# A fused RWKV-style block: the first token mix folded into its weights, Wo's product beside the statistics, spare products, and new orders of all engines

## What is computed

```python
x = x + attn_a(layernorm(x))     # mixer A
x = x + ffn(layernorm(x))        # 8 experts
x = x + attn_b(layernorm(x))     # mixer B
x = x + ffn(layernorm(x))        # the same 8 experts

# attn_a: xx is x one token back
xk, xv, xr = (x * m + xx * (1 - m) for m in (mix_k, mix_v, mix_r))
kv, r = (xk @ Wk.T) * (xv @ Wv.T), xr @ Wr.T
state = kv + exp(time_decay) * state          # a scan over tokens
out = layernorm(r * (time_first * kv + state)) * ln_g + ln_b
return out @ Wo.T

# ffn: every expert on every token, weighted by two softmaxes over experts
h = silu(x @ w_gate[e]) * (x @ w_up[e]);  out = sum_e (h @ w_down[e]) * cw[e]
```

## Time and profile before

| | |
|---|---|
| runs | 925.91, 926.3, 928.23 us; median 926.3 |
| profiled execution | 925.21 us, of it span 923.2 us, mean granted clock 0.972 |
| TensorE busy | 850.2 us (92%), 5170 instructions |
| VectorE | 562.0 us (61%), 927 |
| ScalarE | 401.0 us (43%), 874 |
| GpSimd | 409.2 us (44%), 287 |

### The profile page before, as it was taken

The page is one execution under the profiler, slowest core; times in us unless marked ns, Lnnn a source line. Parts: engine busy times, 40 slices in busy tenths (PEclk is TensorE's granted clock), DMA queues, the critical chain, the costliest instruction groups (busy, mean ns, idle before and its releaser), DMA issues.

```text
span 923.2 us, 13835 instructions
## 1 busy us (share of the span) xinstructions
PE 850.2 (92%) x5170; PEld 717.0 (78%) x5170; DVE 562.0 (61%) x927; ACT 401.0 (43%) x874; POOL 409.2 (44%) x287
## 2 busy tenths in 40 slices
PE   3399999989898999999999799799999799999998
...
DMA packets 20710, 35.87 MB, mean 39 GB/s; under 512 B 3062, under 2 KB 9636, under 8 KB 20644
## 3 DMA queue, kind: packets, MB, share of 16 engines
...
...
## 4 chain that ended last, share of the span: by engine, by line
PE 54%; DVE 9%; issue 2%; ACT 1%; POOL 0%; DVEq 0%; ACTq 0%; POOLq 0%
PE bank L1222 53%; DVE states L1882 1%; DVE sh_buf L1662 1%; DVE w_a L1884 1%; DVE backs L1865 1%; DVE scr L1890 1%; DVE state L1786 0%; PE bank L1236 0%; DVE work L1761 0%; DVE state L1794 0%; ACT sh_buf L1049 0%; ACT w_sb L1137 0%; ACT backs L1121 0%; POOL work L888 0%; DVE stats L1548 0%
## 5 line engine op out<-in xcount | busy, mean ns | idle before, releaser
L1662 DVE TENSOR_TENSOR sh_buf<-sh_buf,bank 128x512 f32<-128x512 f32 x256 | 172.8, 684 | 264.2 <-PE bank L1222 225.6
L1222 PEld LDWEIGHTS bank<-w_down,sh_buf 128*128 128x128 f32 x2048 | 274.9, 193 | 47.9 <-DVE sh_buf L1662 24.7
L1222 PE MATMUL bank<-w_down,sh_buf 128*128 128x128 f32 x2048 | 294.8, 281 | 16.2 <-DVE sh_buf L1662 16.2
L1049 ACT ACTIVATE sh_buf<-bank 128x512 f32<-128x512 f32 x256 | 152.3, 598 | 304.7 <-PE bank L1222 227.9
L1222 PE MATMUL bank<-z_lo,w_hi 128*128 128x512 f32 x512 | 234.5, 458 | 0.9 <-DVE z_lo L1673 0.9
L1222 PE MATMUL bank<-z_hi,w_lo 128*128 128x512 f32 x512 | 204.0, 398 | 0.0
L1222 PE MATMUL bank<-z_hi,w_hi 128*128 128x512 f32 x512 | 203.3, 397 | 0.0
L946 POOL TENSOR_TENSOR x<-x,y_weighted 128x512 f32<-128x512 f32 x63 | 88.5, 1405 | 224.7 <-ACT y_weighted L1163 224.7
L1222 PEld LDWEIGHTS bank<-z_hi,w_hi 128*128 128x128 f32 x512 | 96.9, 189 | 23.4
L1222 PEld LDWEIGHTS bank<-z_lo,w_hi 128*128 128x128 f32 x512 | 98.6, 193 | 14.5 <-issue 3.9
L1222 PEld LDWEIGHTS bank<-z_hi,w_lo 128*128 128x128 f32 x512 | 98.6, 193 | 9.0 <-issue 1.2
...
## 6 DMA issues: line engine op xcount, KB each, us to landing
...
```

Source lines behind the costliest of these rows:

```text
L1049: act.activation(s_buf[:, m % 2, :], bank_of("gate", m)[:], ACT.Silu).then_inc(S["silu_done"], 1)
L1222: return pe.matmul(dst, lhs, rhs, start=start, stop=stop, **kw)
L1662: dve.tensor_tensor(h_buf[:, m % 4, :], s_buf[:, m % 2, :], bank_of("up", m)[:], ALU.mult).then_inc(S["h_done"], 1)
```

## The change

- **Token mix.** For the first batch of unit 0 (s = 0) there is no `mix`. ScalarE scales the three weight matrices of mixer A by the mix and by one minus it (`fold`, six matrices w_mix), and each of k, v and r is two products, one with the tokens and one with the tokens one back. VectorE makes one minus the mix, a centring matrix and a copy of the identity (`fold`). Batches 1 to 3 are as before; GpSimd's first split now waits for the mix of batch 1.
- **Wo.** TensorE makes a centred Wo scaled by ln_g, and ln_b times Wo, once (`output_weights`); ScalarE copies them. `mid_out` multiplies the mixer's result with it directly, with no wait for the norm; `mid_stats` only takes statistics, and `mid_add` applies the factor of each token from PSUM in four scalar_tensor_tensor. The bias is added to x before (`mid_bias`). Centring, scaling, the back transposes and the affine copy are gone for all four blocks.
- **Spare products** on TensorE, whose results nobody reads: 8 before the making of Wo, 8 before the first k, 40 short ones before the first `mid_T`, 28 before the first experts' transposes, 5 before the first gate.
- **Order inside a product.** `split_product` takes z_lo last; the first gate of a pass waits for z_hi, and for z_lo ahead of its last part.
- **Last link.** The 64th link of unit 1 is left out (`last_link`); its result was read by no unit.
- **Orders.** LEAD has new numbers (one list for 64 expert and other groups), as have WEIGHT, CHUNK_TIME and NEAR; PE_SUMS has other steps; the plan's rule for a low clock starts at 45 us (WARM). STICK is 0 and has no effect.

```diff
 LN_EPS_B = 1e-6
...
 WIDE, WIDE_POOL, FULL_POOL, SUM, SUM_STEP = 1.22, 1.95, 2.34, 1.22, 2.05
 PE_SUM = 1.75
-PE_SUMS = dict(T2=[0, 0, 1, 1, 1, 1, 0, 1, 1, 1, 1, 0, 1, 1, 1, 1], W2=[1, 1, 1, 1, 1, 0, 1, 1, 1, 1, 1, 1, 1, 1, 1, 1])
...
 TABLE_LOAD, HOP, START = 1.28, 0.07, 5.0
-CHUNK_TIME = 2.40
-WEIGHT = dict(pe=1.60, act=1.10, dve=1.31, pool=1.10, sp=1.02)
-LEAD = dict(experts=[15.0, -87.7, -93.1, -11.1, -35.5, 8.6, -5.6, 25.5, -52.3, -13.0, -39.8, -122.8, -61.2, -22.7, -10.9, 22.3, -14.4, -56.4, -44.1, -49.8, 37.7, -42.7, 21.0, 9.8, 40.8, 84.3, 89.0, -55.9, -103.9, -34.9, -59.6, 18.9, 76.3, 38.8, -73.9, -81.8, 5.4, 3.3, 25.3, -0.7, -80.3, 79.8, -96.5, -10.0, 41.0, -27.3, 31.4, 42.4, -52.9, 114.6, -88.2, 168.1, -118.3, -81.8, -173.8, 100.3, 113.4, -0.3, -65.5, -148.7, -96.1, 101.2, -151.0, 92.9], front=[-69.8, -115.2, -57.1, 115.0], steps=[62.2, 84.4, -31.2, -8.9], back=[18.5, 79.3, 4.9, 12.1], chain=[-16.1, 67.7], other=[57.8])
...
@@ -133,6 +135,8 @@
...
+        if c == 0:
+            after += (on("dve", "ffn_low", q),)
...
                      *((on("pe", "gate", i // 2 * FC - 9),) if i >= 6 else (on("pe", "r", 1),) if i >= 2 else ()), port=True)]
     return out
...
+            ready += (on("pe", "r", s - 2), on("dve", "inner", s - 2)) if s >= 2 else ()
+            out += [dve(("mix", s), 2.95, *ready, port=True),
+                    pe(("kv", s), 1.87, on("dve", "mix", s), *order, takes=((("k", s), on("act", "kv", s)), (("v", s), on("dve", "scan", s))))]
...
 def middle(q):
+
     u = q // BU
     inner = (on("dve", "inner", 2 * u), on("dve", "inner", 2 * u + 1))
-    out = norm("mid", q, (on("pe", "mid_T", q),), 0.78, (on("pe", "mid_out", q - 1),) if q else (), norm=0.7, centre=False)
-    if q:
...
+            pool(("mid_stats", q), 1.35, on("dve", "mid_stats", q)),
+            pe(("mid_out", q), 0.82, *inner, on("pe", "mid_T", q), on("act", "wo"), *((on("pe", "mid_out", q - 1),) if q else ()), takes=((("mid_out", q), on("dve", "mid_add", q)),)),
+            dve(("mid_bias", q), 0.69, on("act", "wo"), on("dve", "in_centre", q)),
+            dve(("mid_add", q), 0.95, on("pool", "mid_stats", q), on("pe", "mid_out", q), on("dve", "mid_bias", q), *last)]
 
 
 def ffn_input(q):
@@ -228,7 +237,7 @@
     u = j // BU
     z_after = ()
     if j == 0:
-        z_after = (on("dve", "biases"), on("pe", "mid_out", 3), on("pool", "split", 2 * E - 1))
+        z_after = (on("dve", "biases"), on("pe", "mid_out", 3), on("dve", "mid_bias", 3), on("pool", "split", 2 * E - 1))
     elif j == BU:
         z_after = (on("dve", "block_end", j - 1), on("pool", "T4", G * j - 1))
...
 
+def last_link(u):
+
+    return NCH - 1 - (u == UNITS - 1)
...
-            if begin > START + GATE and sum(min(b, begin) - max(a, begin - GATE) for a, b in self.busy) < GATE / 2:
+            if begin > WARM and sum(min(b, begin) - max(a, begin - GATE) for a, b in self.busy) < GATE / 2:
...
-        k_sb, nT = readout[:, 0:BT], readout[:, BT:2 * BT]
+        k_sb = readout[:, 0:BT]
+        spare = z_lo[:, 1, 0:P]
+        wo_centred, wo_bias, centring, wo_scaled = (readout[:, BT + i * C:BT + (i + 1) * C] for i in range(4))
...
+        w_mix = work[:, 0:6 * C].rearrange("p (i c) -> p i c", i=6)
...
+            def mid_scale(q):
+
+                pool.wait_ge(S["mid_mv"], q + 1)
+                step.inc(pool.tensor_scalar(mid_rstd[:, 0, :], mid_mv[:, :, 1], LN_EPS, None, ALU.add))
+                step.wait()
+                pool.tensor_tensor(mid_rstd[:, 1, :], mid_rstd[:, 0, :], neg_half[:].broadcast_to((P, G)), ALU.pow).then_inc(S["mid_rstd"], 1)
...
+            def fold():
+
+                act.wait_ge(S["unmix_rdy"], 1)
+                for i, nm in enumerate(("mix_k", "mix_v", "mix_r")):
+                    step.inc(act.activation(w_mix[:, i, :], w_a[:, i, :], ACT.Copy, scale=col(nm)))
+                    ins = act.activation(w_mix[:, 3 + i, :], w_a[:, i, :], ACT.Copy, scale=unmix[:, i:i + 1])
+                    if i < 2:
+                        step.inc(ins)
+                ins.then_inc(S["folded"], 1)
...
+            def scale_wo():
+                act.activation(wo_scaled, w_a[:, 3, :], ACT.Copy, scale=col("ln_g")).then_inc(S["wo_scaled"], 1)
+
+            def copy_wo():
+                act.wait_ge(S["wo_made"], 1)
+                act.activation(readout[:, BT:BT + 2 * C], bank_of("wo")[:, 0:2 * C], ACT.Copy).then_inc(S["wo_rdy"], 1)
...
+
+                for _ in range(n):
+                    mm(bank[:, 0:P], ident[:], ident[:])
...
+            def keep_busy_short(bank, n):
+
+                for _ in range(n):
+                    mm(bank[:, 0:P], spare, spare)
...
+                take(name)
+                if j == 0 and kind in SPARE:
+                    keep_busy(bank_named[name], SPARE[kind])
                 pe.wait_ge(S["ln_norm"], n + 1)
-                take(name)
...
+            def mixed_product(bank, s, i):
+
+                if s:
+                    return mm(bank, w_a[:, i, :], mixed[s % 2][i])
+                mm(bank, w_mix[:, i, :], xn[:, 0, 1:1 + TU], stop=False)
+                return mm(bank, w_mix[:, 3 + i, :], xn[:, 0, 0:TU], start=False)
...
+                if s == 0:
+                    take(BANK["k", s])
+                    keep_busy(bank_named[BANK["k", s]], 8)
+                    pe.wait_ge(S["folded"], 1)
+                    pe.wait_ge(S["ln_out"], max(LN["in", k] for k in range(BU)) + 1)
+                else:
+                    pe.wait_ge(S["mixed_rdy"], s)
...
-                    ins = mm(bank_named[name][:], w_a[:, i, :], mixed[s % 2][i])
+                    ins = mixed_product(bank_named[name][:], s, i)
...
+                take(name)
+                if q == 0:
+                    keep_busy_short(bank_named[name], 40)
                 pe.wait_ge(S["kvr_used"], B * (u + 1))
-                take(name)
...
+            def output_weights():
+
+                name = BANK["wo",]
+                take(name)
+                keep_busy(bank_named[name], 8)
+                pe.wait_ge(S["unmix_rdy"], 1)
+                pe.wait_ge(S["wo_scaled"], 1)
+                mm(bank_named[name][:, 0:C], centring, wo_scaled)
+                mm(bank_named[name][:, C:2 * C], col("ln_b").broadcast_to((P, P)), w_a[:, 3, :]).then_inc(S["wo_made"], 1)
+                free[name] = (S["wo_rdy"], 1)
...
-                pe.wait_ge(S["ln_out"], LN["mid", q] + 1)
+                pe.wait_ge(S["wo_rdy"], 1)
+                pe.wait_ge(S["kvr_used"], B * (u + 1))
                 take(name)
                 for i in range(G):
-                    ins = mm(bank_named[name][:, i * P:(i + 1) * P], nT[:, i * P:(i + 1) * P], w_a[:, 3, :])
+                    ins = mm(bank_named[name][:, i * P:(i + 1) * P],
+                             oT.rearrange("c (u p i) -> c u i p", u=UNITS, i=LU)[:, u, G * g + i, :], wo_centred)
...
+            def split_product(bank, lo, hi, q, first=False):
+
+                mm(bank, lo, z_hi[:, q % 2, :], stop=False)
+                mm(bank, hi, z_hi[:, q % 2, :], start=False, stop=False)
+                if first:
+                    pe.wait_ge(S["z_low"], q + 1)
+                return mm(bank, hi, z_lo[:, q % 2, :], start=False)
...
+                name = BANK["gate", g]
+                take(name)
+                if g == 0:
+                    keep_busy(bank_named[name], 5)
                 if c == 0:
-                    pe.wait_ge(S["z_low"], q + 1)
+                    pe.wait_ge(S["ln_out"], LN["ffn", q] + 1)
                 if q == 0 and f == 0:
                     pe.wait_ge(S["w_split"], 2 * e + 2)
-                name = BANK["gate", g]
-                take(name)
-                split_product(bank_named[name][:], w_lo[:, e, 0, cols_f], w_hi[:, e, 0, cols_f], q).then_inc(S["g_full"], 1)
+                split_product(bank_named[name][:], w_lo[:, e, 0, cols_f], w_hi[:, e, 0, cols_f], q, c == 0).then_inc(S["g_full"], 1)
...
+            def fold():
+                dve.wait_ge(S["w_in_a"], 16 * 5)
+                dve.wait_ge(S["const"], 2)
+                step.inc(dve.tensor_scalar(centring, ident[:], -1.0 / C, None, ALU.add))
+                step.inc(dve.tensor_copy(spare, ident[:]))
+                step.wait()
+                dve.tensor_scalar(unmix[:], cols[:, COLS.index("mix_k"):COLS.index("mix_k") + 3], -1.0, 1.0, ALU.mult, ALU.add).then_inc(S["unmix_rdy"], 1)
...
-                if b == 0:
+                if b == 0 or s == 1:
                     dve.wait_ge(S["ln_out"], max(LN["in", BU * u + k] for k in range(BU)) + 1)
-                if s == 0:
-                    dve.wait_ge(S["w_in_a"], 16 * 5)
...
+            def mid_statistics(q):
+                dve.wait_ge(S["ot_full"], q + 1)
+                for i in range(G):
+                    ins = dve.bn_stats(mid_stats[:, i, :], inner(q)[:, i, :])
+                    if i < G - 1:
+                        step.inc(ins)
+                step.wait()
```

(28 more changed lines are left out.)

111 lines of the change are left out of this document (62 added, 49 removed).

## The result

| | before | after |
|---|---|---|
| runs, us | 925.91, 926.3, 927.11, 928.23; median 926.7 | 917.1, 917.45, 918.91, 919.09; median **918.18** |
| ratio | | 0.9913, 95% interval 0.9898 to 0.9928 |
| profiled execution | 925.21, span 923.2 | 917.1, span 915.4 |
| first hidden product starts | 49.16 | 42.38 |
| from there to the end of the span | 874.0 | 873.0 |

What follows compares the result with a forecast made beforehand. It took TensorE to bound the body, with holes of a few us, but not the opening. 925.2 - 8.5 (opening) - 2.1 (body) - 1 (orders) = 913.6 profiled; with 1.1 to the median, 914.5 us, range 905 to 921.5.

Steps and rivals of the forecast that it cites:

- Up to the normalised input: Start of the opening: the fold on VectorE costs an estimated 0.45 us; normalised input ready at 14.3 instead of 13.82.
- First token mix: Opening, first k and v products: mix moved into the weights, k's copy at 19.0 against 20.59, 1.65 us earlier.
- GpSimd beside VectorE: First mixer: GpSimd's splits may slow VectorE's steps, 0 to 0.76 us, taken as 0.35; mixer ends at 27.85.
- Middle: From the first mixer's end to z_hi: pieces sum to 8.55 us plus 0.3; z_hi at 36.7, 7.3 earlier.
- sign that I had named: Before the first experts' transposes: forecast is wrong if TensorE runs spare products when the scaled tile is ready.
- z_hi to the first hidden product: VectorE and ScalarE chain with a table load, 43.97 to 49.16, claimed unmoved by the clock; first hidden product 7.3 us earlier.
- Five more wide parts: By the first hidden product TensorE can have five more parts behind it, at 0.24 us each: 1.2 us.
- Body: After the opening: less TensorE work and the last link gain 2.1 us; new orders of all engines taken as -1.
- its two Wo products stay: Unit 1's middle: loses 8 transposes, 0.9 us of TensorE, while the two Wo products remain.
- a body that does not follow: Rival: opening gains as forecast but the body gives back some 5 us: 919 to 923; chance 0.13.
- Rival 2: Body: the new orders take out a quarter of the idle, 904 to 906 us; chance 0.12.
- Rival 3: Opening: clock stays at its lower level and spare products become the bound; first gate 18 us later, 941; chance 0.04.

## Why the prediction was right, and where not

The forecast, faster by the opening, held: 918.18 in a range of 905 to 921.5. It was 3.7 us too low (the sum as written gives 913.6 + 1.1 = 914.7, not 914.5). By its own steps:

1. **Up to the normalised input**: right. The fold stands behind one block's statistics and costs its three short operations; xn is ready at 13.69 (14.3 forecast).
2. **First token mix**: right in kind, 0.9 too late. k's copy 18.10 (19.0 forecast), halves 0.44 apart. The rise of the clock is not fixed: in nine profiles of kernels with the same code up to there k's copy came between 18.10 and 19.35, with 18.51 in the middle. The changed kernel's own is the earliest of them, so 0.4 of the 0.9 is the luck of this execution.
3. **GpSimd beside VectorE**: forecast 0.35, half of the 0.76 for a second step hit. That step was not hit (0.74 at 20.88), the other one was as before (1.52 for 1.50). What was added is in the second scan, 1.71 for 1.23: from k's copy to the mixer's end it takes 9.06 us, before 8.56, so 0.5 in place of 0.35, by another operation than the one named. The mixer ended at 27.16 (27.85). By the Trainium skill, "GPSIMD Engine Reference", section "1. Specifications", the two engines share their interfaces to SBUF, and VectorE's instructions with two SBUF inputs, or in a 2-port mode, contend. The trace agrees, and shows a price well above the 0.76 that I had weighed (1.75 and 2.17 us in the second mixer, in the rows from 513.83 above). The addition of the bias was not hit: two of them take 1.49 us at 11.22, with GpSimd idle.
4. **Middle**: two terms of the sum failed. "They fill that stretch almost to the end, so I add 0.3" is wrong: the spare products cost 0.23 each rather than 0.18 (two halves at the 0.11 of the earlier trace rows, which I used elsewhere, would have given 0.22), and start 4.9 us after the mixer ends rather than 2.9, because a block's Wo product takes 2.06 and not half of the 2.08 that it took at the lower level. So the sign that I had named, spare products running while the scaled tile is ready, is there, and z_hi came at 38.90, not 36.7. The chain of the statistics itself was 1 us longer (tile ready 9.0 after the mixer, 8.05 summed), 0.5 of it GpSimd's first step at 0.73 instead of 0.23.
5. **z_hi to the first hidden product**: "unmoved by the clock. So the first hidden product is 7.3 earlier too" was wrong: it fell by 1.71. I had called it a chain of VectorE and ScalarE and missed that the change itself shortens ScalarE's queue, by the affine copy (with a wait of 1.39) and by zf, which moves behind. And the clock does move it: with the same short queue at the lower level it takes 5.44, no less than before, and the hidden product then waits for TensorE. With the old queue at the upper level it takes 3.90, in part because spare products held z_hi back there by 1.57; with both it is 3.48. That this nearly cancels point 4, 42.38 against a forecast 41.9, is luck.
6. **Five more wide parts**: 1.2 forecast. By the end of the first hidden product TensorE has started 14 against 13, so some 0.2.
7. **Body**: 3.1 forecast, with 6's 1.2 behind the first hidden product 4.3; measured 1.0 in the shortest run, and none in the profile with 18 spare products (874.3 against 874.0 before). The forecast took it from less work of TensorE, with idle and clock unchanged. The traces show the reverse, between the first hidden product and TensorE's last instruction: idle 32.8 us against 39.5, busy 835.7 against 830.0, at the lower level 41.0 against 30.7, which at half speed loses up to 5.1. So without the clock the work is as before (0.6 more), and the lower level takes back most of the 6.7 of idle. Of the terms, "its two Wo products stay" was mis-sized: they stay in number, but in unit 1 too each costs 1.0 more by its strided load, 2.0 against the 0.9 of the removed transposes. "Nothing" for the gates that start before z_lo was too small: about 1 us in the body by the profile with z_lo first. The new orders and one sum fewer, 1 and 0.9 forecast, gave 2.6 to 2.9 together. These parts were measured in different kernels and don't add up exactly.

The rival nearest to the truth was the first, a body that does not follow (919 to 923), for another reason: no wait for a split stands among TensorE's largest; it was TensorE's lower level after idles in the second mixer, as from 745 to 755 us above. Rival 2, a quarter of the body's idle gone, did not occur against the kernel before (36.9 of 40.8 us are left); against the old numbers the new ones take out 10.6 of 47.5, and 7.5 of it come back as busy time. Rival 3, the clock low through the opening, did not occur; its milder form is the run with adjacent columns and 18 spare products.
